# K projection of a Perceiver cross-attention on one core: two of its three row tiles by Strassen's scheme, its 33 tail columns once per tile

## The reference

```
hidden = jnp.concatenate([context, latents], axis=1)     # 257 + 32 = 289 rows
q = (latents @ Wq.T).reshape(b, q_len, H, HD)
k = (hidden @ Wk.T).reshape(b, s_len, KV, HD)            # KV * HD = 384 columns
v = (hidden @ Wv.T).reshape(b, s_len, KV, HD)
scores = jnp.einsum('bkgqd,bksd->bkgqs', q, k) * scale
attn = jax.nn.softmax(scores)
out = jnp.einsum('bkgqs,bksd->bkgqd', attn, v)
return out @ Wo.T
...
_, topk_idx = jax.lax.top_k(channel_map, k)              # k = 20
```

## Time and profile before

| | us |
|---|---|
| median of 3 runs | 2077.06 (2074.2 to 2077.14) |
| the profiled execution | 2076.66 |
| its span in the trace | 2074.5 |
| PE busy | 2021.7 (97% of the span) |
| DVE busy | 1291.7 (62%) |
| ACT busy | 743.1 (36%) |
| POOL busy | 676.0 (33%) |

### The profile page before, as it was taken

One profiled execution on the slowest core, in us unless ns is written; L12 is line 12 of the kernel. 1 busy time (PEld: TensorE's weight loads), 2 busy tenths in 40 slices (PEclk: granted clock), 3 DMA queues, 4 the chain that ended last, 5 costly groups with the idle time before them and its releaser, 6 DMA issues. The chain is left out here.

```text
span 2074.5 us, 36891 instructions
## 1 busy us (share of the span) xinstructions
PE 2021.7 (97%) x11428; PEld 1575.4 (76%) x11428; DVE 1291.7 (62%) x4404; ACT 743.1 (36%) x2046; POOL 676.0 (33%) x1067
## 2 busy tenths in 40 slices
PE   9999999999999999999999999999899999889998
PEld 7878778887887888788787878877566666576665
DVE  4745648475574847557484654847477777667775
ACT  3434334343343434334343433433223232232332
POOL 3323324233332423323242242423233333233332
PEclk9999999999999999999999999999999999999999
DMA  7100001010010101001010100111100000000000
GB/s 286 44 25 25 30 14 31 24 30 24 24 30 15 40 14 31 24 24 30 24 30 17 30 21 24 30 47 41 47 1 1 1 0 0 31 1 21 21 15 26
DMA packets 52573, 62.20 MB, mean 30 GB/s; under 512 B 14258, under 2 KB 48242, under 8 KB 51619
## 3 DMA queue, kind: packets, MB, share of 16 engines
q1 hardware_dynamic: 52514, 61.46, 9.4%
HBM read 54.00 MB, written 4.29 MB: 28 GB/s over the span
## 5 line engine op out<-in xcount | busy, mean ns | idle before, releaser
L438 PE MATMUL psLane<-hid,WkT 128*128 128x289 f32 x1536 | 402.4, 407 | 0.0
L438 PEld LDWEIGHTS psLane<-hid,WkT 128*128 128x128 f32 x1536 | 283.4, 190 | 72.2
L656 ACT ACTIVATE probs<-psLane,nmax 128x289 f32<-128x289 f32 x256 | 126.0, 497 | 430.0 <-DVE nmax L765 430.0
L622 ACT ACTIVATE KT<-psLane 96x289 f32<-96x289 f32 (+2 forms) x384 | 155.5, 405 | 149.9 <-PE psLane L438 147.7
L360 POOL TENSOR_TENSOR w_o<-w_o 128x192 f32<-128x192 f32 x64 | 39.3, 614 | 455.7 <-ACT w_o L631 455.7
L805 DVE MAX8 top<-work 128x8 f32<-128x257 f32 x512 | 180.2, 414 | 2.7
L320 POOL TENSOR_TENSOR tails<-probs,unit 128x66 f32<-128x66 f32 x128 | 38.1, 297 | 437.0 <-ACT probs L656 406.2
L428 PE MATMUL psLane<-xnT,WqT 128*128 128x128 f32 x1536 | 176.7, 275 | 0.0
L428 PEld LDWEIGHTS psLane<-xnT,WqT 128*128 128x128 f32 x1536 | 174.7, 192 | 0.3 <-issue 0.3
L525 PE MATMUL psLane<-WoT,OT 128*128 128x512 f32 x384 | 169.1, 597 | 1.4 <-DVE OT L785 1.4
L790 DVE TENSOR_TENSOR X<-X,psLane 128x512 f32 (+1 forms) x16 | 11.0, 687 | 254.1 <-PE psLane L525 254.1
(11 more groups left out here) (216 smaller groups left out, 4147.7 us busy)
## 6 DMA issues: line engine op xcount, KB each, us to landing
hid<-in_ctxT SPq DMA_DIRECT2D x64, 514.0 KB, 3.8
y<-X SPq DMA_DIRECT2D x16, 256.0 KB, 2.0
X<-in_x SPq DMA_DIRECT2D x1, 3584.0 KB, 21.0
WqT<-in_WqT SPq DMA_DIRECT2D x4, 768.0 KB, 9.3
Vtail<-Vlat SPq DMA_DIRECT2D x128, 24.0 KB
WoT<-in_WoT SPq DMA_DIRECT2D x1, 3072.0 KB, 12.9
w_qkv<-in_w_qkv SPq DMA_DIRECT2D x2, 1536.0 KB, 6.2
w_ffn<-in_w_ffn SPq DMA_DIRECT2D x2, 1024.0 KB, 6.9
```

The costliest lines, as they stand in the source:

```text
L438: mm = pe.matmul(out[:, 0:S], WkT[:, c, P * k:P * k + P], hid[:, j, c, :], start=(c == 0), stop=(c == DC - 1))
L622: ins = act.activation(KT[at:at + hi - lo, j % 2, g, :], psKV[lo:hi, kv_bank(t, 7 * j + k), 0:S], ACT.Copy)
L656: act.activation(probs[:, g, :], psS[:, g % 2, 0:S], ACT.Exp, bias=nmax[:, g:g + 1], scale=XSCALE, accum_out=rsum[:, j % 2, g:g + 1]).then ...
```

## The change

- K's row tiles 0 and 1, for the 256 main columns, are made by Strassen's scheme: seven products of 128 x 128, two matmuls each, with combined weights (`kweights`, four blocks, made once by DVE in `combine_k_weights`) on the left, and blocks of `hid` or V's own row sums `vsums` on the right. They are filled as (1, 2, 5, 4) and (6, 7, 3). Row tile 2 stays four matmuls, now with 256 columns.
- The heads are laid out anew over the row tiles (`PARTS`): heads 0, 1 and 2 are the first 96 rows of row tiles 0, 1 and 2, and head 3 is put together from their last 32 rows.
- ACT copies the products out whole (128x512 and 128x384), POOL adds them into `KT` with seven operations of 128x128 (`k_first`, `k_second`, `k_third`), and ACT copies head 3's rows and the tail columns into place (`finish_k`); the scores wait for that (`kt_ready`).
- The last 33 columns of K (the last context row and the 32 latents) are made once per tile for all four batches: `k_tail`, 12 matmuls with 132 columns, between the `q` calls. `evac_xt` writes their operand `xnK` instead of `hid`, with one more copy of 128x16 for the last context row.
- POOL: `sum_rows` comes ahead of `gather_tails`, since K needs the sums too, and `add_second` comes behind it.
- DVE, in batch 3 of a tile: step 8 of batch 2's top-k comes behind the row maximum, and `evac_ot` comes ahead of top-k step 1.
- PE: `q` 2 comes behind values 3. In tile 0 the first scores no longer wait until q 2 has been copied out.
- The scratch data lies in `w_qkv`, so the load of that weight for the next part now waits for K of the last batch. Tile 0 makes its row sums ahead of V's combined weights. Three semaphore increments that nobody waited for are gone.

```diff
+K_FILLS = ((1, 2, 5, 4), (6, 7, 3), ())
+TAIL_FILLS = ((0, 1), (2,))
...
+            def k_first(t, j):
+                pool.wait_ge(kv_evac, kv(t, 7 * j) + 1)
+                wait(pool, s_filled, 2 * (TB * t + j) - 2)
+                pool.tensor_tensor(k_block(j, 0, 0), k_product(1), k_product(2), ALU.add).then_inc(k_ready, 1)
...
                 for j in range(TB):
-                    gather_tails(t, j, 0)
                     if j < TB - 1:
                         sum_rows(t, j + 1)
+                        if j:
+                            add_second(t, j)
+                        gather_tails(t, j, 0)
+                        k_first(t, j + 1)
+                        k_second(t, j + 1)
+                        k_third(t, j + 1)
...
             def k_part(t, j, k):
                 out = next_bank(t, 7 * j + k)
+                sums_made = 4 * (TB * t + j)
                 if k == 0:
                     pe.wait_ge(ctx_in[j], 16 * (t + 1))
-                    pe.wait_ge(m_evac, m_xt(t) + 1)
-                for c in range(DC):
-                    mm = pe.matmul(out[:, 0:S], WkT[:, c, P * k:P * k + P], hid[:, j, c, :],
-                                   start=(c == 0), stop=(c == DC - 1))
+                if k == 2:
+                    for c in range(DC):
+                        mm = pe.matmul(out[:, 0:MAIN], WkT[:, c, 2 * P:3 * P], hid[:, j, c, 0:MAIN],
+                                       start=(c == 0), stop=(c == DC - 1))
+                for i, n in enumerate(K_FILLS[k]):
...
+                    if n == 5:
+                        pe.wait_ge(vsum_step, sums_made + 1)
+                    if n == 6:
+                        pe.wait_ge(vsum_step, sums_made + 4)
+                    mm = k_product(out[:, P * i:P * i + P], j, n)
+                mm.then_inc(kv_filled, 1)
...
             def evac_xt(t):
...
                 dve.tensor_copy(xnT[:].rearrange("p c q -> p (c q)"), psM)
-                dve.tensor_copy(hid[:, :, :, CTX:S], psM.rearrange("p (c j q) -> p j c q", c=DC, j=TB))\
+                dve.tensor_copy(xnK[:, :, :, 0], clast[:, :, bass.ts(t, TB)])
+                dve.tensor_copy(xnK[:, :, :, 1:TAIL], psM.rearrange("p (c j q) -> p c j q", c=DC, j=TB))\
                    .then_inc(m_evac, 1)
...
                     row_max(t, j, 0)
+                    if j == TB - 1:
+                        topk(t, j - 1, 8)
+                        evac_ot(t, j - 1)
                     topk(t, j, 1)
-                    if j:
+                    if 0 < j < TB - 1:
                         evac_ot(t, j - 1)
                     if j == TB - 1 and not last:
                         evac_xt(t + 1)
```

More of the change, by code:

```diff
@@ L278, in body @@
                 if last:
-                    for k, name in (("w_qkv", "w_qkv0"), ("loraA", "loraA"),
+                    for k, name in (("loraA", "loraA"),
                                     ("cos", "cos"), ("sin", "sin"), ("causal", "causal"), ("block16", "block16"),
@@ L389, in body @@
                             sum_rows(t + 1, 0)
[L390 to L396, removed]
+                        gather_tails(t, j, 1)
             rstd_of(0)
+            sum_rows(0, 0)
             combine_weights()
-            sum_rows(0, 0)
             over_tiles(pool, body)
@@ L423, in q @@
             def q(t, k):
-                out = next_bank(t - 1, 29 + k)
+                out = next_bank(t - 1, kv_q(k))
                 for r in range(G):
@@ L430, in q, with k_product @@
                 mm.then_inc(kv_filled, 1)
+            def k_product(out, j, n):
+                columns = lambda s, k: lambda c: hid[:, j, 2 * k + c, P * s:P * s + P]
+                summed = lambda i: lambda c: vsums[i][:, c, :]
+                block = lambda k, n: lambda c: WkT[:, 2 * k + c, P * n:P * n + P]
+                combined = lambda i: lambda c: kweights[:, i, c, :]
+                left, right = {1: (block(0, 0), columns(0, 0)), 2: (block(1, 0), columns(0, 1)), 3: (block(1, 1), summed(3)),
+                               4: (combined(3), columns(1, 1)), 5: (combined(0), summed(0)), 6: (combined(1), summed(1)),
+                               7: (combined(2), summed(2))}[n]
+                for c in range(2):
+                    mm = pe.matmul(out, left(c), right(c), start=(c == 0), stop=(c == 1))
+                return mm
@@ L440, in k_part, with k_tail @@
+            def k_tail(t, f):
+                out = next_bank(t - 1, kv_tail(f))
+                pe.wait_ge(m_evac, m_xt(t) + 1)
+                for i, k in enumerate(TAIL_FILLS[f]):
+                    for c in range(DC):
+                        mm = pe.matmul(out[:, TAILS * i:TAILS * i + TAILS], WkT[:, c, P * k:P * k + P],
+                                       xnK[:, c].rearrange("p j n -> p (j n)"), start=(c == 0), stop=(c == DC - 1))
                 mm.then_inc(kv_filled, 1)
@@ L553, in body @@
                     pe.wait_ge(wq_in, 64)
-                    for k in range(NKT):
-                        q(0, k)
-                    pe.wait_ge(kv_evac, kv(-1, 31) + 1)
+                    q(0, 0)
+                    k_tail(0, 0)
+                    q(0, 1)
+                    k_tail(0, 1)
+                    q(0, 2)
                 else:
@@ L602, in body @@
                         else:
+                            k_tail(t + 1, 0)
                             q(t + 1, 1)
-                            q(t + 1, 2)
+                            k_tail(t + 1, 1)
                     values(t, j, 2)
                     values(t, j, 3)
+                    if j == TB - 1 and not last:
+                        q(t + 1, 2)
                 if first:
@@ L677, in body @@
                 if first:
-                    for k in range(NKT):
-                        evac_q(0, k)
+                    evac_q(0, 0)
+                    evac_k_tail(0, 0)
+                    evac_q(0, 1)
+                    evac_k_tail(0, 1)
+                finish_k(t, 0)
+                if first:
+                    evac_q(0, 2)
                 for j in range(TB):
@@ L881, in body @@
                         evac_ot(t, j)
-                    for step in range(5 if j == TB - 1 and last else 3, 9):
+                    for step in range(5 if j == TB - 1 and last else 3, 8 if j == TB - 2 else 9):
                         topk(t, j, step)
```

122 lines of the change are left out of this document (102 added, 20 removed).

## The result

The changed kernel takes 2062.66 us (median of 4 runs, 2062.48 to 2064.01), the kernel before, measured beside it, 2076.95 (4 runs, 2074.2 to 2077.14). The ratio is 0.9939, with a 95% interval of 0.9925 to 0.9953: by the medians 14.3 us less, twice the 7.0 that were forecast. The profiled execution took 2064.01 us, with a span of 2062.2 against 2074.5.

The account below looks back on a forecast made before the run. PE, busy for 97% of the span, was taken to bound the kernel. K with tails -20.6, v_latents wait +12.1, tile 0 +0.3 and last tile +1.2 gave -7.0 us: 2070 from 2077.06, range 2056 to 2078.

Parts of the forecast that it names:

- the two large terms: PE's matmul time for K with the tails, -20.6 us in 16 tiles, and waiting at v_latents, +12.1 us.
- rival B: Batch 3 of a tile: no new wait at v_latents; 2058, or 2051 at the faster column rate; chance 0.22.
- K's term: K's row tiles on PE: 4.85 us instead of 5.85, 1.00 less a batch.
- the other bound: K's products at the 289-column rate, 0.108 us each: a batch saves 1.10 us, 27.6 us in all.
- The tails: K's tail columns, once per tile on PE: 24 instructions at 0.113 us, 2.71 us added.
- The new wait at v_latents: Batch 3: PE waits for DVE's later copies, 0.83 us in tiles 1 to 14, 0.46 if the copy isn't held.
- Tile 0: Start of the cross-attention: 1.28 us idle goes, waits for q 2's bank and K's product 4 come; net +0.3 us.
- the main term: K's shorter batches less the tails: PE has 1.29 us less a tile, 20.6 us less in 16 tiles.
- Last tile: Tile 15: the last two heads' turn waits for exponentials made later by DVE's second row maximum; +1.2 us.
- rival C: DVE late in batch 2, small operations held beside POOL; 10 us more, 2080; chance 0.20.
- a sign of being wrong: Batch 3: row maxima later than 1.17 us behind their scores would show the forecast wrong.
- rival D: POOL's new chain holds PE in every batch, by sums or second tails; at 0.3 us a batch, 2089; chance 0.13.

Follow-up runs that it names:

- experiment 3: Kernel before, with ScalarE's first copy of transposed probabilities ahead of the copies of K's second row tile in batches 0 to 2; 2070.21 us, ratio 0.9969.
- experiment 1: Changed kernel with VectorE's old order in a tile's last batch (mask ahead of row maximum, copy of O behind first top-k step); 2065.03 us, ratio 0.9940.
- experiment 2: Kernel before with only VectorE's new order in a tile's last batch; 2083.66 us, ratio 1.0032.
- experiment 6: Changed kernel, in the last tile only: second top-k step of the last batch behind the second row maximum; 2061.70 us.
- experiment 8: Changed kernel with two more GpSimd additions in each batch, written to memory that nothing reads; 2066.58 us.
- experiments 4: Changed kernel with the small 128x16 copy moved into VectorE's idle time ahead of the copy of O transposed; 2055.26 us, ratio 0.9894.
- 5: Changed kernel with small copy moved, copies of xn ahead of first top-k step, last tile's second top-k step behind second row maximum; 2050.68 us, ratio 0.9875.
- 7: Changed kernel with the small copy moved and VectorE's old order put back in the last batch; 2067.09 us.

## Why the prediction was right, and where it was short

The time lies in the range, and the two large terms came as forecast; the sum was still short by half, for a gain that it did not have. That this gain fitted into the range is luck in part: the fast end had been put there for rival B, a missing wait at v_latents, and that wait came.

**K's term, -1.00 us a batch: right.** 28 products at 0.112 us, the third row tile 1.76 for 1.73, and 1.00 us a batch between experiment 3 and the changed kernel. The 0.108 of the other bound did not come. The tails are 2.71 us to the digit.

**The new wait at v_latents: right in place, mechanism and size.** Forecast +0.83 us a tile, scores to v_latents 7.1; measured +0.73 and 7.04, in 15 tiles. Its two parts are shown one at a time: without the small copy 0.44 us a tile go, without the MAX ahead the last 0.26. What makes the copy dear is shown too: at the same place in the program it takes 0.55 us where it meets POOL's row sum and 0.17 in experiment 1, where it does not. By the Trainium skill (SBUF — State Buffer, Who interferes with whom) such a copy and a GpSimd instruction lock each other out; the trace agrees, with 0.55 us beside POOL's sums (mean of 14) against 0.18 without.

**The term that was missing: values 0.** The sum has no term for ACT's order around the first transposed probabilities, because I looked there only for what the change could make late. The row that shows it, the weight load with 0.26 us of waiting for ACT's probsT, was in the trace of before. It is worth 0.35 us a tile by the trace of experiment 3, 5 to 6 us in 16 tiles (6.7 by its medians), most of the 7.3 us by which the forecast fell short.

**Once only.** Tile 0: the first scores stand at 38.4 to 39.4 us in the seven traces with the change's start, 35.7 to 36.8 in the three with before's; means 38.7 and 36.25, +2.5 us. Of these 2.71 are the tails and -1.00 the K of one batch, which the main term already counts, so about +0.8 is left for +0.3 forecast; the traces of either group differ by up to 1 us there. Last tile: +1.2 forecast; experiment 2 shows 1.65 - 0.43 = 1.22, experiment 6 gives 1.0 back.

**DVE in batch 2 (rival C): half true.** Its small operations are held beside POOL: in the lists by line, nmax goes from 169 to 250 ns and top_last from 261 to 330 (means of 128 and 64). The row maximum of batch 3 comes 1.32 us behind its scores instead of 1.17, which the prediction had named as a sign of being wrong; PE loses only 0.1 us by it (4.80 instead of 4.70 us from the first to the second scores). Rival C did not come because the mask stood behind the row maximum: with it ahead (experiment 1) it comes, 0.56 us a tile, and the mask itself takes 0.59 us there beside POOL instead of 0.23.

**POOL (rival D): not there.** Its adds take 0.46 us, as I had put them (two of the seven 0.53 and 0.56 in the mean), and experiment 8 shows the room.

**The sum with measured sizes.** K and the tails -20.6, the wait +10.9 (15 x 0.73), tile 0 +0.8, the last tile +1.2, values 0 -5.6 (16 x 0.35): -13.3 us, against 14.3 less by the medians.

**What stays open.** The parts of the profiled spans add to -12.3 us (start +1.8, from there to the last batch -16.3, last batch to the end of this stage +1.2, the rest +1.0). The rest of the program is the same and differs by 0 to 1.1 us between the traces, for a reason that stays open.

## What to carry to other kernels

Where one engine is busy for 97%, look for the small stalls between its instructions before counting what a change removes: stalls of 0.06 to 0.22 us in three batches of a tile are in no table of waits, and a two-line reordering on another engine gave 6.7 us, a third of the 20.6 that the new algebra takes off PE. When a stage gets shorter, the order of the engine that feeds it has to be found again: the same order of VectorE cost 6.7 us in the one kernel and nothing in the other, where the medians even lean its way by 2.4. Put the work that somebody waits for first, even where the engine then idles, and small copies where GpSimd is quiet.

## What the runs showed of the hardware

**A lock that lasts.** In tile 0 one addition on POOL of 128x128, elsewhere 0.45 us, took 7.30 beside VectorE's build-up of the bands. The timelines of POOL and DVE of the kernel after:

```profile
19.75 7.30 POOL L374 TENSOR_TENSOR w_qkv<-w_qkv 128x128 f32<-128x128 f32 x1
...
20.30 6.43 DVE L984 SCALAR_TENSOR_TENSOR band<-work,taps,band 128x384 f32<-128x384 f32 x12
```

It ends at 27.05, just behind DVE's last one (26.73). PE did not wait for it: the first scores, which need K, start at 38.5, and K's last addition on POOL ends at 28.3.

**The clock dips once in the last tile, not always at the same place.** The table of stretches of the kernel after (length, then busy us of PE, PEld, DVE, ACT and POOL, granted clock, DMA share, GB/s):

```profile
1425.00:1430.00 5.00, 3.65 (x16) 2.09 (x15) 3.02 (x11) 2.00 (x7) 0.30 (x1) 0.79 0.84 318
1430.00:1435.00 5.00, 5.00 (x15) 2.92 (x14) 0.00 (x0) 0.00 (x0) 0.00 (x0) 0.86 0.24 102
```

and of the kernel before, where the same products ran at 1.00 and the projection behind them did not:

```profile
1450.00:1455.00 5.00, 4.04 (x6) 1.89 (x7) 4.31 (x20) 0.00 (x0) 0.00 (x0) 0.66 0.00 0
```

After, the eight products behind the 1.31 us wait took 5.05 us for 3.63 and the projection's 24 took 10.57; before, 3.63 and 12.17: 15.6 against 15.8 in sum, so the dip costs the change nothing. (0.66 to 0.86 are means over 5 us in which the clock stood for a part at 1.2 instead of 2.4 GHz.) But it is not a simple price of a wait: in experiment 2 PE waited 1.65 us there and both ran at full clock, 3.63 and 10.57, as they did in experiment 6 without that wait. Of the ten traces three have the slow stretch at the eight products (after, experiments 4 and 8), five at the projection (before, 1, 3, 5 and 7), and two have none. Those two, of experiments 2 and 6, are the fastest executions of their kernels (2080.94 of a median of 2083.66, 2060.98 of 2061.70), so it may well differ from one execution to the next of the same kernel; one trace of each kernel cannot show that.
